# Two Mamba layers with a tree and eight experts: the D term moves onto the mask's diagonal, halos move to GpSimd, work at the layers' border is put in another order, and x is turned ahead of z

## The reference, cut to what matters

```python
# a mixer, both layers (8 heads of 64 and 3 taps in the first, 4 heads of 128 and 4 taps in the second)
zxbcdt = u @ in_proj
z, xBC, dt = split(zxbcdt)
dt = softplus(dt + dt_bias)
xBC = silu(causal_depthwise_conv(xBC))        # looks back taps - 1 tokens: the halo
x, B, C = split(xBC)
state = state * exp(dt * A) + dt * x * B      # token by token
y = C . state + D * x                         # D: one number per head
out = rmsnorm(y * silu(z)) @ out_proj
# the experts of the second layer
scores = softmax(xt @ Wr);  G, idx = top_k(scores.T, 1024)
out = zeros.at[idx].add(G * mlp_e(xt[idx]))
```

## Time and profile before

| | |
|---|---|
| median of 3 runs | 1469.93 us (1469.26 to 1473.24) |
| the profiled execution | 1473.88 us, its span 1472.2 us |
| mean granted clock of TensorE | 0.97 |
| busy: PE, DVE, ACT, POOL | 95%, 72%, 53%, 33% |
| chain that ended last, by engine | PE 76%, DVE 12%, ACT 5% |

### The profile page before, as it was taken

How to read it: one execution, slowest core, us unless ns; L and a number is a source line. 1 busy time by engine, 2 the same in 40 slices (tenths; PEclk the granted TensorE clock), 3 DMA queues, 4 the chain that set the end, 5 groups by cost and what they waited for, 6 DMA issues and landing times.

```text
span 1472.2 us, 23472 instructions
## 1 busy us (share of the span) xinstructions
PE 1397.6 (95%) x7578; PEld 1058.7 (72%) x7578; DVE 1053.1 (72%) x2493; ACT 774.6 (53%) x1612; POOL 487.6 (33%) x599
## 2 busy tenths in 40 slices
PE   7889999999999999999789999999999999999996
PEld 4567768686777768676555655565688898889895
DVE  7889685868769686846589889899865646564642
ACT  4263443526262543526377766887765655465552
POOL 1343334342414234340112221122423544354333
PEclk9799999999999999999799999999999999999998
DMA  7110211203030201211511121121133533343322
GB/s 233 56 58 30 88 43 44 87 0 123 6 108 21 101 28 44 72 35 39 175 40 52 56 69 45 68 73 55 49 82 94 116 74 62 98 108 79 59 46 29
DMA packets 71867, 100.95 MB, mean 69 GB/s; under 512 B 13017, under 2 KB 58209, under 8 KB 71777
## 3 DMA queue, kind: packets, MB, share of 16 engines
q1 hardware_dynamic: 59488, 82.77, 17.3%
q0 software_dynamic: 12288, 17.05, 6.8%
HBM read 74.30 MB, written 25.49 MB: 68 GB/s over the span
## 4 chain that ended last, share of the span: by engine, by line
PE 76%; DVE 12%; ACT 5%; issue 4%; POOL 1%; PEldq 0%; DMA 0%; SPq 0%; DVEq 0%; PEld 0%; ACTq 0%; POOLq 0%
PE bank L2266 70%; DVE am L1753 3%; DVE u L1753 2%; PE bank L2378 1%; DVE E L1773 1%; PE bank L2679 1%; PE bank L2404 1%; DVE hits L2000 1%; PE bank L2621 1%; PE bank L2343 1%; DVE yb L2109 1%; ACT am L1155 1%; ACT tg L1116 1%; PE bank L2560 1%; PE bank L2465 1%
## 5 line engine op out<-in xcount | busy, mean ns | idle before, releaser
L2225 DVE TENSOR_TENSOR aml<-m0big,amh 128x512 fp32r<-128x512 f32 x128 | 88.1, 689 | 175.9 <-ACT amh L1436 175.8
L1033 POOL DMA_INDIRECT out<-EW,IDX x64 | 103.7, 1620 | 219.6 <-DVE EW L2220 205.0
L1431 ACT ACTIVATE m0big<-bank,eb 128x512 f32<-128x512 f32 x128 | 87.9, 687 | 162.4 <-PE bank L2266 146.7
L2266 PE MATMUL bank<-w2h,amh 128*128 128x256 f32 x512 | 147.9, 289 | 0.0
L2266 PE MATMUL bank<-w2h,aml 128*128 128x256 f32 x512 | 144.7, 283 | 0.0
L2266 PE MATMUL bank<-w2l,amh 128*128 128x256 f32 x512 | 144.7, 283 | 0.0
L2266 PE MATMUL bank<-EW,am 128*128 128x256 f32 x512 | 115.8, 379 | 0.0
L1155 ACT ACTIVATE am<-bank,b 128x512 f32<-128x512 f32 x64 | 43.5, 682 | 126.8 <-PE bank L2266 126.1
L2266 PEld LDWEIGHTS bank<-EW,am 128*128 128x128 f32 x512 | 97.2, 190 | 13.5 <-ACT am L1155 0.3
L2266 PEld LDWEIGHTS bank<-w2h,amh 128*128 128x128 f32 x512 | 97.6, 191 | 8.3 <-issue 5.8
L960 POOL TENSOR_TENSOR Xs<-Xsb,lp 128x512 f32<-128x512 f32 x32 | 40.5, 1265 | 188.1 <-ACT Xsb L1207 188.1
(11 more groups left out here) (349 smaller groups left out, 3644.2 us busy)
## 6 DMA issues: line engine op xcount, KB each, us to landing
EW<-in_e_w SPq DMA_DIRECT2D x16, 1024.0 KB, 6.2
dA0b<-dA_d SPq DMA_DIRECT2D x16, 512.0 KB, 3.8
E<-dA_d SPq DMA_DIRECT2D x16, 512.0 KB, 5.3
m0big<-dA_d SPq DMA_DIRECT2D x16, 512.0 KB, 4.8
xin<-in_L_attn_x SPq DMA_DIRECT2D x8, 512.0 KB
xp<-in_L_attn_x SPq DMA_DIRECT2D x8, 512.0 KB, 3.8
rows_d<-xo SPq DMA_DIRECT2D x8, 512.0 KB, 3.1
x_d<-xb SPq DMA_DIRECT2D x8, 512.0 KB, 4.1
```

The lines of the kernel that those rows point to most:

```text
L1033: g.indirect_dma_start(out=out_rows, out_offset=bass.IndirectOffsetOnAxis(ap=IDX[:, 4 * u + c:4 * u + c + 1], axis=0), in_=ye[:, q, c, :], ...
L1431: a.activation(am2[:, j % 2, :], bank[j % 2][:, :], ACT.Gelu, bias=eb1[:, u // 2, j:j + 1]).then_inc(gelu_sig.sem, 1)
L2225: v.tensor_tensor(aml[:, j % 4, :], am2[:, j % 2, :], amh[:, j % 4, :], ALU.subtract).then_inc(am_low.sem, 1)
L2266: return t.matmul(out_, lhsT, rhs, start=first, stop=last)
```

## The change

It has five parts. In the second layer D is no longer multiplied into x: ACT writes a diagonal matrix of D once (`XD`, from `ident`), POOL adds it to each tile's mask (`diagonal1`), and the masked product then holds the D term; PE's `intra1` waits for that add in place of the mask. ACT's four instructions and DVE's add per tile are gone. POOL does the halo copies (`halos1`, in the third iteration of a step). The 15 threshold rounds stand at tiles 2 to 20, none at tile 1, and DVE's constants, score copy and first count stand behind its sums of tile 0. PE turns z and x of tile 1 ahead of the transposes of the last norm. In the first layer PE and ACT take x ahead of z in the tiles 1 to 3 of a step.

```diff
-        ROUNDS = {1: 0}
-        ROUNDS.update((n, 3 * (n // CH) + n % CH - (n % CH > 0)) for n in range(2, 5 * CH) if n % CH != 1)
+        ROUNDS = dict(zip([n for n in range(2, TILES1) if n % CH != 1], range(15)))
...
+            def halos1(i):
+                for j in range(5):
+                    blk = (j - 1) % 5
+                    s1.u.wait_ge(pool, i, j + 1)
+                    if i % (STEPS // NB) == STEPS // NB - 1:
+                        ins = g.memset(xbuf[:, blk, 0:3], 0.0)
+                    else:
+                        ins = g.tensor_copy(xbuf[:, blk, 0:3], xbuf[:, blk, T:T + 3])
+                    ins.then_inc(s1.halo.sem, 1)
+
+            def diagonal1(i, c):
+                s1.M.wait_ge(pool, i, c + 1)
+                s1.xd.wait_ge(pool, 0, 1)
+                e = E[:, c % 2, 0:512]
+                g.tensor_tensor(e, e, XD[:, 0, :], ALU.add).then_inc(s1.Dd.sem, 1)
...
             xrows1(0, 0)
+            diagonal1(0, 0)
+            halos1(0)
...
                 if n + 1 < TILES1:
                     xrows1(*divmod(n + 1, CH))
+                    diagonal1(*divmod(n + 1, CH))
                 if n + 2 == TILES1:
                     gather(0, 0, 2)
                 if n:
                     y_rms1(*divmod(n - 1, CH))
+                if n % CH == 2 and n + CH < TILES1:
+                    halos1(n // CH + 1)
...
+                if c == 0:
+                    z_silu()
                 p = front_wait(act, L, s, i, f"xt{c}")
                 s.xdt.wait_ge(act, i, c - 1)
                 s.xd.wait_ge(act, i, c - 1)
                 a.activation(Xsb[:, q, :], p[:, :], ACT.Copy).then_inc(s.xsb.sem, 1)
+                if c:
+                    z_silu()
...
-                s1.xsb.wait_ge(act, i, c + 1)
-                for k in range(NH1):
-                    ins = a.activation(XD[:, q, P * k:P * (k + 1)], Xsb[:, q, P * k:P * (k + 1)], ACT.Copy,
-                                       scale=W[1]["D"][:, k:k + 1])
-                ins.then_inc(s1.xd.sem, 1)
...
-                s1.u.wait_ge(dve, i, j + 1)
-                if i % (STEPS // NB) == STEPS // NB - 1:
-                    v.memset(xbuf[:, blk, 0:3], 0.0).then_inc(s1.halo.sem, 1)
-                else:
-                    v.tensor_copy(xbuf[:, blk, 0:3], xbuf[:, blk, T:T + 3]).then_inc(s1.halo.sem, 1)
...
-                s1.xd.wait_ge(dve, i, c + 1)
-                op(v.tensor_tensor(yb[:, q, :], yb[:, q, :], XD[:, q, :], ALU.add))
...
-            count(0)
+            def first_count():
...
+                count(0)
...
                 sums1(i, c)
+                if n == 0:
+                    first_count()
...
                 if c == 0:
+                    z_rows()
                     s.xc.wait_ge(pe, i, 6)
                 p = open_front(pe, L, s, i, f"xt{c}")
                 for k in range(CH):
                     last = t.transpose(p[:, cols(k)], s.u_buf[:, k, cols(c)], ident[:, :])
                 filled(last, s, L, f"xt{c}")
+                if c:
+                    z_rows()
...
                     in_proj1(0, 0)
+                else:
+                    z_xt1(0, 1)
...
-            z_xt1(0, 1)
...
-                s1.M.wait_ge(pe, i, c + 1)
+                s1.Dd.wait_ge(pe, i, c + 1)
```

More of the change, by code:

```diff
@@ L444, in program @@
         s1.half = sig(n + "inter_half", CH)
-        s1.E, s1.M, s1.rv = (sig(n + name, CH) for name in ("decays", "mask_ready", "y_var"))
+        s1.E, s1.M, s1.rv, s1.Dd = (sig(n + name, CH) for name in (
+            "decays", "mask_ready", "y_var", "diagonal_added"))
         mv_sig = sig("var_ready")
@@ L1120, in chunk, with z_silu @@
                 q = c % 2
-                p = front_wait(act, L, s, i, f"z{c}")
-                s.yg.wait_ge(act, i, c - 1)
-                a.activation(zs[:, q, :], p[:, :], ACT.Silu).then_inc(s.zs.sem, 1)
+                def z_silu():
+                    p = front_wait(act, L, s, i, f"z{c}")
+                    s.yg.wait_ge(act, i, c - 1)
+                    a.activation(zs[:, q, :], p[:, :], ACT.Silu).then_inc(s.zs.sem, 1)
+                if c == 0:
+                    z_silu()
                 p = front_wait(act, L, s, i, f"xt{c}")
@@ L1304, in step0 @@
                     chunk1(0, 0)
+                    for k in range(NH1):
+                        ins = a.activation(XD[:, 0, P * k:P * (k + 1)], ident[:, :], ACT.Copy,
+                                           scale=W[1]["D"][:, k:k + 1])
+                    ins.then_inc(s1.xd.sem, 1)
                     decay_exps1(0)
@@ L1982, in _ @@
                           ident[0:64, 64:P].unsqueeze(1).to_broadcast([64, 8, 64])).then_inc(bias_steps.sem, 1)
[L1983 to L1989, removed]
             def count(n):
@@ L2159, in low_w2 @@
                 v.tensor_tensor(w2l[:, sl, :], ws2[:, sl, :], w2h[:, sl, :], ALU.subtract).then_inc(w2_low.sem, 1)
-            count(0)
+            def first_count():
+                op(v.tensor_reduce(Q8, ident[:, :].rearrange("p (a b) -> p b a", b=NE), AXX, ALU.add))
+                v.tensor_copy(G8.rearrange("p (a b) -> p a b", b=NE),
+                              Q8.unsqueeze(1).to_broadcast([P, P // NE, NE])).then_inc(prepped, 1)
+                s1.sct_full.wait_ge(dve, 0, 1)
+                v.tensor_copy(SCT, YO[:, 0:256]).then_inc(s1.sct.sem, 1)
+                s1.sct.wait_ge(dve, 0, 1)
+                dve.wait_ge(prepped, PREPPED + 9)
+                count(0)
             for n in range(TILES1):
@@ L2333, in chunk, with z_rows @@
                 q = c % 2
[L2334 to L2337, removed]
+                def z_rows():
+                    p = open_front(pe, L, s, i, f"z{c}")
+                    for k in range(KD):
+                        last = mm(p[:, :], s.hT_buf[:, k, cols(c)], w["z"][:, k, :], k == 0, k == 1)
+                    filled(last, s, L, f"z{c}")
                 if c == 0:
+                    z_rows()
                     s.xc.wait_ge(pe, i, 6)
```

## The result

The changed kernel takes 1475.3 us (median of 12 runs, 1473.24 to 1480.61), the kernel before 1469.53 us (12 runs, 1467.98 to 1473.24). The ratio is 1.0038, with a 95% interval of 1.0026 to 1.0051: slower by about 5.8 us, where 1460.5 had been forecast. The profiled execution took 1473.55 us, its span 1471.8. All ratios are of fast executions alone: one slow execution each of after_norm_first (2182.40 us) and halos_back (3691.37) and two of the kernel before on their chip (1545.17 and 4788.14) are left out, though the medians printed for the two runs, 1469.09 and 1455.89, still count them (1468.93 and 1455.48 without).

The account below looks back on a forecast made before the run. PE was taken to bound the first layer, DVE's part of each step and PE the second mixer. The terms summed to -9.45 us on the profiled 1473.88, or 1460.5 against the median 1469.93; range 1452 to 1475.

Parts of the forecast that it names:

- x ahead of z: First layer: PE's wait for the state at tile 2 comes bare, 1.95 us in each of seven steps, +13.7 us.
- the second mixer: Second layer's mixer: PE's waits for DVE's state shrink (-9.75, -0.2) and the clock behind them is given back (-10.8 us).
- the tail: End of the second mixer: gathers stand behind the last tile's add on GpSimd and PE waits for their rows, +1.0 us.
- the border: Between the layers: z and x of tile 1 fill a wait (-2.9 us), the new round order saves more (-2.5 us).
- rival 3: First layer: the bare wait also costs PE's clock; +24 us if in all seven steps, 1484 us; chance 0.11.
- What it delays is y's norm: Second mixer: GpSimd's added add delays the norm and output by some 0.7 us, where DVE waits for PE anyway.
- rival 2: Second mixer: clock not given back, or the third tile's later norm and Xs hold DVE; +10.8 us, 1471.3; chance 0.20.
- the -0.2 for the wait: Second mixer, step 4: the last threshold round's counts, 1.71 us, now precede PE's wait, leaving a gain of only 0.2 us.
- the 2.45 behind it: Second mixer, steps 1 to 4: the tile behind the shortened wait runs at full clock, 2.45 us gained in each.
- Rival 1: First layer: GpSimd and DVE take turns otherwise, bare wait only 1.1 us a step, -6 us more, 1454.5; chance 0.12.
- rival 5: Second mixer: DVE's gain doesn't reach PE, as ACT or the projection sets the state's time; +10 us, 1471; chance 0.05.
- Rival 4: Second mixer: GpSimd's added adds hold DVE 0.85 us each; three tiles in seven steps +18 us, 1478; chance 0.06.

Follow-up runs that it names:

- after_norm_first: The changed kernel with GpSimd making y's norm ahead of its add of D, x still ahead of z: 1469.09 us, ratio 0.9985 to the kernel before.
- halos_back: norm_first with the halo copies on DVE again: 1455.89 us, ratio 0.9881 to the kernel before.
- norm_first: The changed kernel with z ahead of x again and y's norm ahead of GpSimd's add: 1446.54 us, ratio 0.9827; repeated (_2) 1444.19 us, 0.9824.
- x_alone: The kernel before with only x ahead of z in the first layer: 1493.98 us, ratio 1.0151.
- x_tile2_only: The changed kernel with z ahead of x in the first layer again, except at tile 2: 1461.68 us, ratio 0.9941 to the kernel before.

## Why the prediction was wrong

Of the 14.8 us between 1460.5 and 1475.3 the traces place 9.05: the first layer came out 3.2 us worse than forecast (8.5 us of lost clock, against a first step that was 6 us better than forecast), the second mixer 5.5 worse, the tail 2.0 worse and the border 1.6 better. The other 5.7 are the base that the sum was set on.

**What bounds the kernel** held: PE in the first layer, and in the second mixer DVE's part of a step, seen as one wait.

**x ahead of z: direction and bare waits right, the clock missing.** The wait, its place, its releaser and its size came as worked out (13.7 us forecast for seven steps, 14.0 measured), and so did the indirect way over GpSimd's Xs (0.85 taken for the scans, 0.80 measured). The step that failed is that "1.95, since DVE has stood for GpSimd in both places" was priced as bare waiting alone: the +13.7 held nothing for the clock behind the wait, which was kept as rival 3, at 0.11, against a row that showed 1.97 us to be enough. It happened five times of seven, 8.5 us. Rival 3 had the mechanism, but took the stretch at 6.8 us and so each loss at 3.4; here they were 3.41 and 1.7.

**The first step** was put at +2; up to tile 0 of step 1 the traces show 106.58 against 110.57, -4. Since two traces of one kernel differ by as much, that is no reading of the change.

**The second mixer: -20.75 forecast, -15.3 measured.** The steps with a full gain came out better than forecast: from the wait of step 0 to that of step 3 12.5 us, where 10.75 were forecast, since the halos were mis-sized (net 0.1 us each in the sum, 0.5 a step; by halos_back 1.0 to 1.4 us a step in these). In the steps 1 to 3 the wait fell to 0.44 us, by 2.2 to 2.9, and the clock was given back. What failed is "What it delays is y's norm [...] where DVE waits for PE anyway". DVE did not wait for PE there: its output stood ahead of work that PE was to wait for, and in the last tiles the norm closed a ring. From tile 16 on 1.65 us were gained where 8.05 were forecast: the last two tiles cost 1.6 us more, the stretch of 13.10 us in step 4 0.7 more, and in that step the wait grew to 3.02 us where 1.75 was forecast, and the tile behind it stayed at half clock (11.45 us). This was the second half of rival 2, and it should have been worked out by listing the mask, the add, the norm and the output in one line. With the norm ahead the clock of step 4 is still lost: there the wait is 1.95 us (908.77 in norm_first_2), as long as it was before, so the -0.2 for the wait came out as nothing, and the 2.45 behind it, which rested on a wait of 1.75, did not come.

**The tail**: +1.0 forecast, +3.0 measured, +1.7 with the norm ahead; the order of norm and add cost here too. The add itself was put at 1.04 us, the time of `XD`, and takes 1.27.

**The border**: -5.4 forecast, -7.0 measured. The direction and the place were right, the size was within the bounds.

**The base**: the sum went against one profiled execution, and its distance to the median (3.95 us) was carried over to the result. The other kernel's execution stood 1.75 us on the other side of its median. The two distances together are the 5.7 us that the terms don't explain. The parts measured alone add up to 1.51 - 0.24 - 1.10 = +0.17% by their ratios, 2.5 us, with intervals that reach to the +0.38% of the whole. What in the changed kernel's other executions takes the 1.75 us over its trace, beyond the scatter of the first step, no run here settles.

**The other rivals.** Rival 1 fell with the 3.79 us of the scans, rival 5 with the waits that shrank. Rival 4 had a sign but no part in the result: DVE's gate is 0.87 us beside the add in most tiles, for 0.68, and in norm_first it is 1.50 to 1.72 in ten tiles, yet norm_first runs at PE's pace in the last tiles and is the faster kernel. The gate stands behind the state add that PE waits for.

## What to carry to other kernels

A wait that an added instruction causes is found by walking the queue that it is put into: whoever stands behind it is later by its whole length, and the one who waits for that one may be ahead of the instruction's own input; if so, a ring is closed, and each tile pays. Put the small result that others wait for ahead of the large one that is needed an iteration later.

An independent product ahead of a waiting one is cover. Before it is moved behind, read when the awaited result comes, and count what a bare wait of that length has done to the clock elsewhere in the same trace as part of the price, not as a rival.

A version with z ahead of x, D on the diagonal and the norm ahead of the add (norm_first) takes 1444 to 1447 us, ratio 0.9824 and 0.9827, 1.75% below the kernel before and 2.1% below the change.

## What the runs showed of the hardware

- Whether a wait of PE costs the clock is not set by its length alone near 2 us: of the five waits of 1.97 us in the changed kernel three were followed by half clock and two (steps 2 and 5) were not, the same ones in after_norm_first, while in x_alone the steps 3 and 6 were spared; 1.75 us cost it in halos_back and 1.82 did not; 1.0 to 1.2 us in x_tile2_only never did. What decides among waits of one length no run here settles.
- The stretch at half clock behind such a wait was 3.41 us each time in the first layer and mostly 6.83 us in the second mixer (770.92 to 777.75 in the changed kernel; 3.41 at 1024.63 in the kernel before), so the price was 1.7 us in the one and up to 3.4 in the other.
- GpSimd's `Xs` (a product of 128x512) takes 1.04 us at its shortest and 1.93 us where all of it lies beside DVE's scans, and these take 0.80 us longer: both engines lose.
